# A decoder layer on one core: both ends of the state-space block, both seams and the final norm rearranged

## What is computed

```
# 1 state space (N = 16 states, D = 256 channels)
Xn = layernorm(x)
X_main = silu(causal_conv(Xn @ W_up1.T, 4 taps) + conv_b)
pp = X_main @ W_ll.T + b_ll ; delta = softplus(pp[:D]) ; Bm, Cm = pp[D:D+N], pp[D+N:]
A_bar = exp(delta * A) ; U = X_main * (A_bar - 1) / (delta*A) * delta * Bm
H = A_bar * H + U (along the tokens) ; Y = sum_n Cm * H
x = layernorm(x + x + (Y * silu(Xn @ W_up2.T)) @ W_down.T + b_down)
# 2 cross-attention with context, 16 heads, on layernorm(x) and layernorm(ctx)
x = layernorm(x + attention)
# 3 six layers: local attention in windows of 32 tokens, tokens shifted by one, feed-forward
x = layernorm(x0 + six_layers(x0))
```

## Time and profile before

| what | us |
|---|---|
| median of 3 runs | 2393.26 |
| those runs | 2393.24, 2393.26, 2395.58 |
| the profiled execution | 2395.99 |
| its span, first to last instruction | 2394.1 |
| state-space block in it | 0 to 322 |
| cross-attention block | 322 to 625 |
| window layers | 625 to 2378 |
| final norm and store | 2378 to 2394.1 |

### The profile page before, as it was taken

One profiled execution on the slowest core, in us unless ns is written; L12 is line 12 of the kernel. 1 busy time (PEld: TensorE's weight loads), 2 busy tenths in 40 slices (PEclk: granted clock), 3 DMA queues, 4 the chain that ended last, 5 costly groups with the idle time before them and its releaser, 6 DMA issues. The chain is left out here.

```text
span 2394.1 us, 69394 instructions
## 1 busy us (share of the span) xinstructions
PE 2235.1 (93%) x26001; PEld 1466.8 (61%) x26001; DVE 1861.7 (78%) x2679; ACT 1704.1 (71%) x3296; POOL 1648.7 (69%) x1552
## 2 busy tenths in 40 slices
PE   5899879999699999999999999999999999999995
PEld 3555446666356666666666666666666666666663
DVE  4899957777578878888888887888887888888873
ACT  5889734544377787777777777778778777777772
POOL 4777832322378778787787787877877878778771
PEclk8999999999899999999999999999999999999996
DMA  2312210000022222222222222222222222222220
GB/s 73 112 59 68 71 47 1 1 1 1 21 62 67 54 78 66 63 68 66 72 60 67 78 53 69 75 53 78 66 54 77 66 63 68 66 72 60 67 77 27
DMA packets 102908, 140.36 MB, mean 59 GB/s; under 512 B 63040, under 2 KB 63936, under 8 KB 102336
## 3 DMA queue, kind: packets, MB, share of 16 engines
q1 hardware_dynamic: 102848, 139.57, 21.4%
HBM read 56.39 MB, written 1.31 MB: 24 GB/s over the span
## 5 line engine op out<-in xcount | busy, mean ns | idle before, releaser
L1760 PE MATMUL f_psA<-f_W,f_xT 128*128 (+1 forms) x1152 | 601.5, 631 | 20.1 <-DVE f_m L1586 11.4
L1586 DVE TENSOR_TENSOR f_m<-f_psA,f_tab 128x1024 f32<-128x1024 f32 x384 | 461.5, 1222 | 128.1 <-ACT f_sq L1452 114.0
L1345 POOL TENSOR_TENSOR f_Pr<-f_Pr,f_rden 128x384 f32<-128x384 f32 x384 | 310.7, 830 | 234.9 <-DVE f_rden L1565 234.9
L1373 POOL TENSOR_TENSOR f_qkr<-f_qkr,f_rn 128x1024 f32<-128x1024 f32 x192 | 361.5, 1904 | 0.2 <-POOL f_rn L1381 0.2
L1760 PEld LDWEIGHTS f_psA<-f_W,f_xT 128*128 128x128 f32 x1152 | 188.7, 190 | 163.4 <-issue 109.2
L1452 ACT ACTIVATE f_sq<-f_psA 128x512 f32<-128x512 f32 x384 | 228.1, 594 | 81.4 <-PE f_psA L1760 78.8
L1731 PEld LDWEIGHTS f_psO<-f_PT,f_V 96*64 96x64 f32 x6144 | 203.5, 138 | 96.2 <-issue 89.2
L1363 POOL TENSOR_TENSOR f_qkr<-f_m 128x512 f32<-128x512 f32 x192 | 244.5, 1273 | 14.4 <-DVE f_m L1586 14.4
L1364 POOL TENSOR_TENSOR f_qkr<-f_m 128x512 f32<-128x512 f32 x192 | 244.6, 1274 | 0.0
L1731 PE MATMUL f_psO<-f_PT,f_V 96*64 96x64 f32 x6144 | 231.8, 227 | 1.6 <-ACT f_PT L1427 1.5
L791 POOL TENSOR_TENSOR x_Es<-x_E 128x512 f32<-128x512 f32 x64 | 81.1, 1267 | 205.6 <-DVE x_E L896 205.6
(11 more groups left out here) (168 smaller groups left out, 4876.1 us busy)
## 6 DMA issues: line engine op xcount, KB each, us to landing
f_V<-f_Vt SPq DMA_DIRECT2D x96, 384.0 KB, 4.2
f_V<-f_Vt SPq DMA_DIRECT2D x96, 256.0 KB, 3.6
f_W<-in_f_W SPq DMA_DIRECT2D x48, 344.0 KB, 3.2
m_Cb<-m_BC_rows SPq DMA_DIRECT2D x64, 256.0 KB, 3.1
f_W<-in_f_W SPq DMA_DIRECT2D x48, 296.5 KB, 4.2
f_V<-f_Vt SPq DMA_DIRECT2D x48, 128.0 KB, 5.3
f_xsA<-xall SPq DMA_DIRECT2D x97, 32.0 KB
f_xsA<-xall SPq DMA_DIRECT2D x97, 31.8 KB
```

The costliest lines, as they stand in the source:

```text
L1345: pool.tensor_tensor(pv, pv, rv.unsqueeze(3).broadcast_to([P, 2, 2, KEYS]), ALU.mult).then_inc(Pr_ready[g][j], 1)
L1373: pool.tensor_tensor(qv, qv, rv.unsqueeze(3).broadcast_to([P, 2, GH, DH]), ALU.mult).then_inc(qkr_ready[g], 1)
L1586: dve.tensor_tensor(m12[:, j, :, half].rearrange("p m (h d) -> p m h d", d=DH), psA[n % 2][:, :].rearrange("p (h d) -> p h d", d=DH).unsqu ...
L1760: pe.matmul(psA[n % 2][:, :], xT[:, t, :], weights(i, W_QKV + n * 512, 512), start=True, stop=True).then_inc(A_full[n_fill], 1)
```

## The change

Five places change; the loop body of the window layers does not.

- **Start of the state-space block.** `hats(0)` goes from POOL to DVE, and so do step 0's `rounding` and `delta`, which now stand in DVE's own list. Step 0's gates (two matmuls, two silus) come last on PE, and ACT does them in slot 0, between two table loads. The banks of PSUM are given out in that order. `exp(A_log)` is written in place.
- **Heads of steps 1 to 3.** LEAD is 23. Pieces up to k=12 come a slot sooner, pieces from 14 on stay in their slot (their k is one more). The gates are in halves: c=0 at k=12, c=1 at k=13 on PE, and on ACT the silus of xc at 12, both gates at 13. `tokens_of_BC` comes a slot later, with `one_plus(i, 0)` right behind it.
- **End of the state-space block.** `first_rows_of_cross` (statistics and hats of the cross block's batch 0) stands on DVE behind unit 63, its 1/sigma on ACT beside it; `finish(3)` goes from POOL to DVE. The cross block starts with PE's transposes.
- **Seam to the window layers.** The cross block issues tile 0's two shift transfers when batch 0 is finished; SP and PE do not wait for `setup` any more before the first slot, and ACT copies `x0` behind slot (0, 0).
- **Final norm.** Three parts, tiles 0 to 9, 10 to 13, 14 and 15, each stored by itself. Parts 0 and 1 are done between the last slots.

```diff
@@ state_space_block
-    LEAD = NST + 6
+    LEAD = NST + 7
-        fills = [(0, n) for n in FILL_NAMES]
+        fills = [(0, n) for n in FILL_NAMES if n[:3] != "up2"] + [(0, "up20"), (0, "up21")]
@@ gpsimd
-            hats(0)
...
-            for c in range(NC):
-                rounding(0, c)
-                delta(0, c)
...
-                if r == 5:
+                if r == 5 and i < STEPS - 1:
                     finish(i)
@@ scalar
+                if g == 0:
+                    silu_gates(0)
...
                     if k == 12:
                         silus(i)
+                    if k == 13:
+                        silu_gates(i)
@@ vector
+            def first_rows_of_cross():
+                dve.wait_ge(cross.loaded, CROSS_LOADS)
+                dve.wait_ge(res_ready, 3)
+                rows = [xall[:, j, :] for j in range(TPB)] + [cross.ctxall[:, j, :] for j in range(TPB)]
+                layer_norm_stats(dve, passed, mom_ready, chain, rows, cross.stats, cross.mom)
+                dve.wait_ge(rstd_ready, STEPS + 1)
+                for n, row in enumerate(rows):
+                    dve.tensor_scalar(cross.hat[:, n, :], row, cross.mom[:, n, 0:1], cross.rstd[:, n:n + 1], ALU.subtract, ALU.mult)
...
-                    if k == 14:
+                    if k == 16:
                         tokens_of_BC(i)
+                        one_plus(i, 0)
...
+                if g == UNITS - 1:
+                    first_rows_of_cross()
@@ cross_attention_block, sync
             window.load(sp)
+            sp.wait_ge(finished, 1)
+            window.shift_first_tile(sp, xall)
@@ window_layers
+    PARTS = [(0, 10), (10, 14), (14, 16)]
...
+            slot(ITERS, 0, "BCD")
+            final_moments(0)
+            slot(ITERS, 1, "CE")
+            final_rows(0)
+            final_moments(1)
+            slot(ITERS + 1, 0, "D")
+            final_rows(1)
+            slot(ITERS + 1, 1, "E")
+            final_moments(2)
+            final_rows(2)
```

203 lines of the change are left out of this document (127 added, 76 removed).

## The result

The changed kernel takes 2382.3 us, the median of 5 runs (2380.69 to 2383.33); the kernel before took 2393.26 beside it. The ratio is 0.9952, with a 95% interval of 0.9937 to 0.9966. That is 11.0 us gained where 25.6 were forecast, and outside the range of 2361 to 2374.

A forecast was written before the change was run, and what follows sets the result against it. PE was taken to bound the window loop, DVE the state-space block, and bare chains the seams and tail. -0.4 + 3.7 + 5.3 + 7.0 + 10.0 = 25.6 off the median 2393.3 gave 2367.7 us, range 2361 to 2374.

The forecast's parts named there:

- likeliest case: Whole kernel: the forecast with its own ends, 25.6 us gained, time 2367.7; chance 0.52.
- Start: State-space start: unit 0 some 3.2 us sooner, spent again behind ACT's gates; net -0.4, ends -1.5 and +2.
- Middle: Steps 1 to 3: tokens_of_BC a slot later fills DVE's waits, less one_plus meeting times_C; +3.7, ends 0 and +7.5.
- gross 6.0: Steps 1 to 3: gains of 2.6, 1.3 and 2.1 us, before the charge for one_plus meeting POOL.
- rival 1: POOL and DVE shut each other out wherever they meet: middle 0, tail 7.5, start -1.0; sum 18.8, time 2374; chance 0.15.
- rival 3: ACT becomes the bound in the middle through load pairs: middle -2, start -1.5; 2374 to 2379 us; chance 0.07.
- Seam 1: State-space block's end: hats on DVE, PE's cross-block transpose at 320.3 instead of 325.60; +5.3, ends +4 and +7.2.
- Seam 2: Seam to the windows: tile 0 shifted early, PE starts at about 625.35 instead of 632.47; +7.0, ends +5 and +7.3.
- Loop: Window layers: PE-bound with unchanged body, so 0 counted and the same 35.5 us a turn expected.
- Rival 5: Window loop entered in another phase between SP's transfers and engines, so longer turns; 2404 us at 0.8 a turn; chance 0.02.
- Drain: Last slots behind the loop: final_rows(0) delays the last gated by 0.45, hatC meeting DVE charged 0.6; -1.1.
- Tail: Behind the last addition: two-tile chain and small store, 4.9 us instead of 16.0; 11.1 gained, +10.0 after charges.

The follow-up runs named there:

- e1: Changed kernel with step 1's 1/sigma ahead of step 0's gates in ACT's list; 2379.89 us, 0.9932 of the kernel before.
- e7: Changed kernel with one_plus on ACT behind its exp instead of on DVE, loop's place held by padding; 2374.48 us, 0.9913 of the kernel before.
- e8: Changed kernel with both gates of a step at k=12 again, two table loads less in each of steps 2 and 3; 2380.08 us, 0.9938 of before.
- e9: Changed kernel with window layers, seam into them and final norm as before; only state-space block and first seam changed; 2398.86 us, 1.0011 of before.
- e3: Kernel before with only the change's seam to the window layers; 2388.76 us, 0.9972 of the kernel before.
- e13: Kernel before with 18 small DVE memsets at the cross block's start, its loop at instruction 1192 as in the changed kernel; 2402.10 us, 1.0029 of before.
- e4: Kernel before with only the change's final norm in three parts; 2384.45 us, 0.9953 of the kernel before.
- e5: Kernel before with DVE's list 2 instructions longer ahead of the loop, by split semaphore increments; 2394.13 us, 0.9995 of before.
- e12: Changed kernel with 1/sigma first, one_plus on ACT, gates together, cross hats behind gated(3), part 0's moments behind POOL's last f_Pr; 2371.89 us, 0.9902 of before.

## Why the prediction was wrong

The likeliest case was 25.6 us, and 11.0 came. 4.3 of the difference are no term: I took 25.6 off a median that lay 2.7 below its profiled execution, and the changed kernel's median lies 1.6 above its own. The profiled executions differ by 15.3. The other 10.3 are these.

- **Start: +0.6 for -0.4, within its ends.** The 1/sigma of step 1 came at 46.90 where I had 47.5, and the units were held up as described; e1 shows that the gates' place was the cause, some 2 us at unit 3. The difference of 1.0 is less than what the kernels with these same instructions scatter at unit 8.
- **Middle: the term was mis-sized, +3.7 forecast and -0.6 measured.** The gross gain was there: DVE does not wait at `tokens_of_BC` any more. The failed step is "I charge 1.5 for `one_plus(i, 0)` in each of three steps, but take only half of the sum off". Not three but five of the six became long, and together they cost 11.63 - 4.24 = 7.4 us more, where I took off 2.3. The traces split the -0.6: up to unit 63, e7 shows 5.7 gained on the kernel before when these instructions are not on DVE, near my gross 6.0; with them 5.5 are spent again, and the four hats ahead of `gated(3)` take 0.75. This is the mechanism of rival 1. I had set it aside because "other `one_plus` next to POOL's work take 0.40", and that was a misreading of the kernel before: its 0.40 at 86.86 began 0.17 ahead of POOL's `times_C` (87.03), and its 0.58 at 95.84 ended 0.28 behind one that ended at 96.14. No row there spoke against it. The -0.6 itself is small: of the six kernels with the block of before, four need 236.9 to 237.1 from unit 8 to `gated(3)`, two 238.5 and 238.6. By the Trainium skill, "SBUF — State Buffer", section "🔬 SBUF: two separate sides", the later of the two engines blocks for the whole instruction of the other; the rows of 2.17 and 1.87 that end 0.3 us behind POOL agree, and by that rule the lower end of my term, 0, was the one to take. ACT's extra loads, rival 3, cost little: e8 gets back 0.7 us of the middle without them.
- **Seam 1: the chain was right, the number in part luck** (5.2 for 5.3). In five kernels with the same instructions the projection down ran at the lower level and the seam gave 3.5 to 3.7, below my lower end of 4; I had counted the clock as a possible gain only. And the hats of the cross block that I put into the idle 4.50 took 3.5 us beside POOL and not 1.1. I had named POOL's `times_C` as something to wait for, not to meet.
- **Seam 2: right** (7.2 for 7.0).
- **Loop: the failed step is "the change leaves its body alone, and so I count nothing there".** It cost 5.9 us. Rival 5 named a longer turn, by SP's transfers and PE's phase, and gave it 0.02; what makes it longer is neither. e9 has it without the earlier start, e3 has the earlier start without it, and e13 makes it in the kernel before with 18 memsets. Of the 5.9, 46 turns of 0.106 are 4.9. The other 1.0 lies in the first turns, and stays open: from PE's first transpose to the 12th `ssq` the runs scatter from 195.6 to 198.1 without an order that I can see. The clock is a part of it, with a granted 0.89 over the first 75 us after and 0.92 before.
- **Drain: -2.3 for -1.1.** 1.3 of it go with PE's clock at the exit of the loop. e4 has the same instructions behind the loop and the full clock at the exit, and its drain takes 59.7, 1.0 more than before, as forecast; with the lower level it takes 61.0 in the changed kernel. The difference is there from the exit on: the next row `f_x<-f_psO` of DVE starts 23.3 behind the last `ssq` instead of 22.0. That the level is the whole cause is not shown, since e5 and e13, with before's instructions and the lower level, need 59.0 and 57.5, where before needs 58.7. So the 1.0 was right in size but not in its reason. The meeting that I charged to `hatC` hardly was there, POOL took 0.88 for it instead of 0.80; another was, part 0's addition with `f_Pr` (2.49 for 1.62). e12, with that addition moved and the full clock, needs 59.2, 0.5 less than e4.
- **Tail: right** (11.2 for 11.1). The store's part had a wrong step that hardly counts: 4.27 - 2.35 and an eighth of 2.35 are 2.2 and not 2.4. No run shows its 440 GB/s either: in the kernel before, the 1 MB moved from 2390.7 to 2393.4, some 390 GB/s. The store of 128 KB ends 2.35 behind its issue at 2376.55.

## What to carry to other kernels

Before an instruction moves on VectorE, look at what GpSimd runs at its new place: an instruction of 0.4 us that lands beside one of 2.4 us lasted here until that one ended, and a filled hole is worth nothing if the same length is paid behind it. When a short row speaks against such a meeting, compare the two starts first: it may simply have begun earlier. A loop whose body is untouched is not free of the change: compare the length of a turn in both traces, and if it differs, shift the loop in its engine's list. A median and a profiled execution are two samples, and a range should be widened by their distance. Runs that share the instructions of a stretch tell how much that stretch scatters; compare a new trace with all of them and not with one.
